# A cleared tile and a wait after every gather of node rows in a four-layer graph network

## The reference, cut to what matters

```python
edge_index = jnp.stack([src, dst])
h = jnp.maximum(_layernorm(x, axis=-1), 0.0)
x = x + _L0_gnn_ref(h, L0_gnn_weight, src, dst, edge_type_16)   # one matrix per edge type, summed by dst
h = jnp.maximum(_layernorm(x, axis=-1), 0.0)
x = x + _L1_gnn_ref(h, edge_index, L1_gnn_Wl, L1_gnn_Wr, L1_gnn_b)   # mean of neighbours, 3 steps
...
x = x + _L2_gnn_ref(h, L2_gnn_weight1, L2_gnn_weight2, src, dst)     # rows scaled by degrees
...
x = x + _L3_gnn_ref(h, edge_index, ...)                              # attention over neighbours, 2 steps
return x
```

## Time and profile before

| What | us |
|---|---|
| Median of three runs | 6565.89 |
| The three runs | 6560.53 to 6572.52 |
| Span of the profiled execution, first to last instruction | 8635.1 |
| Busy in it: DVE / POOL / PE / ACT | 4326.1 / 4305.3 / 4016.2 / 2282.2 |

### The profile page before, as it was taken

The page is one execution under the profiler, slowest core; times in us unless marked ns, Lnnn a source line. Parts: engine busy times, 40 slices in busy tenths (PEclk is TensorE's granted clock), DMA queues, the critical chain, the costliest instruction groups (busy, mean ns, idle before and its releaser), DMA issues. The chain is left out here.

```text
span 8635.1 us, 76490 instructions
## 1 busy us (share of the span) xinstructions
PE 4016.2 (47%) x19708; PEld 2671.9 (31%) x19708; DVE 4326.1 (50%) x14882; ACT 2282.2 (26%) x5999; POOL 4305.3 (50%) x4026
## 2 busy tenths in 40 slices
PE   1111158312888825654563664342465476567000
PEld 0000034101555514443442443332344355233000
DVE  3010069301999944434432553565244698677553
ACT  0000000001777621110110333354111133799000
POOL 5777720575000046546555674774555100888577
PEclk8555589655999955555555555555666666798555
DMA  1111100000222222222222343343122144555222
GB/s 42 47 46 47 47 19 0 21 1 5 103 113 107 99 70 79 69 73 64 69 68 63 112 128 112 94 139 112 44 68 68 77 161 163 125 146 138 76 82 77
DMA packets 413612, 684.96 MB, mean 79 GB/s; under 512 B 283685, under 2 KB 290444, under 8 KB 407978
## 3 DMA queue, kind: packets, MB, share of 16 engines
q1 hardware_dynamic: 282410, 542.14, 17.7%
q0 software_dynamic: 130944, 140.05, 7.5%
HBM read 310.94 MB, written 373.78 MB: 79 GB/s over the span
## 5 line engine op out<-in xcount | busy, mean ns | idle before, releaser
L711 POOL DMA_INDIRECT G<-states,srcq x1568 | 1678.9, 1071 | 851.1 <-issue 479.5
L1133 DVE TENSOR_TENSOR_SCAN R<-same,R,G 128x28 f32<-128x28 f32 x4480 | 883.8, 265 | 622.1 <-issue 499.9
L1793 PE MATMUL PS<-ident,HH 128*128 128x128 f32 x2357 | 529.8, 376 | 1257.4 <-ACT AT L2063 373.2
L2063 ACT COPY AT<-PS 128x512 f32<-128x512 f32 (+1 forms) x494 | 283.7, 581 | 2467.3 <-remote 1375.1
L1793 PEld LDWEIGHTS PS<-ident,HH 128*128 128x128 f32 x2357 | 402.8, 205 | 1332.9 <-issue 409.9
L711 POOL DMA_INDIRECT EE<-node_info,srcq x392 | 394.4, 1006 | 545.0 <-DMA node_info<-XC 415.7
L1701 PE MATMUL PS<-R 128*128 128x392 f16 x784 | 283.0, 361 | 673.2 <-remote 375.7
L711 POOL DMA_INDIRECT G<-states,srci x392 | 406.7, 1038 | 321.0 <-ACT HH L2161 199.1
L1808 PEld LDWEIGHTS PS<-WD,AT 128*128 128x128 f32 x2358 | 505.8, 316 | 183.0 <-issue 182.7
L1808 PE MATMUL PS<-WD,AT 128*128 128x64 f32 x2358 | 560.6, 416 | 0.0
L824 POOL DMA_INDIRECT out_nodes<-O,dstq x392 | 430.9, 1099 | 188.2 <-issue 123.3
(11 more groups left out here) (412 smaller groups left out, 10157.6 us busy)
## 6 DMA issues: line engine op xcount, KB each, us to landing
states<-O SPq DMA_DIRECT2D x70, 896.0 KB, 3.6
HH<-states SPq DMA_DIRECT2D x56, 896.0 KB
total<-R SPq DMA_DIRECT2D x56, 896.0 KB
XB<-resid SPq DMA_DIRECT2D x42, 896.0 KB
states<-HH SPq DMA_DIRECT2D x28, 896.0 KB, 3.9
G<-states,srcq POOLq DMA_INDIRECT x1568
resid<-XB SPq DMA_DIRECT2D x28, 896.0 KB
xl_of_src<-O SPq DMA_DIRECT2D x14, 1792.0 KB
```

What stands on the lines that cost most here:

```text
L711: return pool.indirect_dma_start(to, None, table_, bass.IndirectOffsetOnAxis(ap=idx, axis=0), bounds_check=bound, oob_is_err=False).then_i ...
L1133: last = dve.tensor_tensor_scan(out=out_[:, order, f], data0=flags[:, order], data1=in_[:, order, f], initial=initial[:, f:f + 1], op0=ALU ...
L1793: last = pe.transpose(PS[:, 4 + k, q * P:(q + 1) * P], HH[:, b, (g * G4 + q) * D2:(g * G4 + q + 1) * D2], ident[:])
L2063: act.copy(AT[:, k, 0:n * P], PS[:, 4 + k, 0:n * P]).then_inc(s_copied, 1)
```

## The change

A spare tile of 64 columns (32 KB, 256 bytes in each partition) is made. After each of the 784 gathers of node rows and each of the 392 gathers of node records GpSimd clears it and waits, with `step`, until the clearing is done, before it goes on to the next gather. That is 1176 clearings and as many waits. Nothing reads the tile. The gathers of the layers are as they were.

```diff
@@ -148,6 +148,7 @@
         fw = sb("fw", [P, 2, 6, HCOLS])
+        idle = sb("idle", [P, 64])
@@ -713,6 +714,9 @@
+            def pause():
+                step(pool.memset(idle[:], 0.0))
+
@@ -792,6 +796,7 @@
                 for j in range(PC):
                     at = turn % PCHUNKS * PC + j
                     gather(PG[:, b, j * D:(j + 1) * D], x, idx[:, at:at + 1], N - 1, s_pg[b])
+                    pause()
                     if j == PC // 2 and turn:
                         keep_rows(turn - 1)
```

## The result

The changed kernel takes **7335.84 us** (median of 4 runs, 7320.55 to 7341.27), the kernel before, run beside it, 6564.61 us (4 runs, 6560.53 to 6572.52). The ratio is 1.1174, with a 95% interval of 1.1158 to 1.119: 771 us slower (760 to 781). The forecast was 7319 us.

A forecast was written before the change was run, and what follows sets the result against it. The prediction took GpSimd's line of gathers to bound the preparation before layer 0, and added 1176 pauses of 0.64 us, 753 us, to the median 6566 us, giving 7319 us, range 6760 to 7570 us.

The forecast's parts named there:

- No stretch in the timed runs: Before layer 0, the trace's slowing of DVE beside GpSimd's gathers, 1480 us, was taken to be absent from the timed runs.
- The balance of the parts: Whole kernel without the stretch: 1630 us before layer 0 + 5527 - 559 = 6598 us, 0.5% from the median.
- GpSimd's line bounds the preparation, DVE's some tens of us to either side: Before layer 0, GpSimd's gathers end at 1625 us and set its start; DVE's line arrives together, at about 1630 us.
- the 50 us kept for that: Before layer 0: if DVE's line is now the later one, up to 50 us of the pauses is absorbed.
- The clearing, 0.14 us, right behind the gather: In each pause on GpSimd, clearing 64 columns takes 0.14 us and starts at once at the gather's end.
- The wait, 0.80 us instead of 0.30: In each pause, the next gather starts 0.80 us after the clearing's end, against 0.30 us between gathers today.
- The sum, 0.64 us x 1176 = 753 us: On GpSimd's line before layer 0, the period grows from 1.30 to 1.94 us, all on the path; chance 0.72.
- What else could be late: Edge stage: destinations' rows land at 891 us, DVE's last sum at about 1746 us, hidden under GpSimd's 2378 us.
- The SBUF port at nothing: Clearings beside DVE's histogram wait for none of its operations: nothing added; rival with 97 us more, 7416 us, chance 0.05.
- The cheap wait: Rival: the next gather is prepared ahead as far as the wait; 0.21 us a pause, 6813 or 6763 us; chance 0.14.
- The relief of a stretch: Rival: the stretch is real in timed runs and pauses let the histogram run under the gathers; 5883 us, chance 0.06.
- the hidden pause: Rival: DVE's timed line ends past 2378 us, so the pauses cost nothing; 6566 us, chance 0.03.

The follow-up runs named there:

- the second profile of before: The kernel before, unchanged, profiled once more: 6569.48 us, span 6567.8 us.

## Why the prediction was right

The forecast held: 7319 us, measured 7335.84. By its steps:

- **No stretch in the timed runs.** Right. The balance of the parts that led there came out well partly because two errors cancelled: it put layer 0 at 1633 us and all behind it at 4968, and the second profile of before shows 1723.6 and 4843. The record-keeping of the profile alone does not make the stretch: the profile of after and those of the nine experiments, with the same kind of records, have spans like their timed runs. That agrees with the Trainium skill, "NOTIFIC — the notification-queue block", section "10. Constraints, capacities, measured rates", by which a trace record costs the engine no cycles. What stretched that one execution is not known.
- **GpSimd's line bounds the preparation, DVE's some tens of us to either side.** Right, and the side is settled: DVE ended 47.7 us earlier. So nothing of the change was absorbed, and the 50 us kept for that were not needed. The line itself was mis-sized: 1625 us were forecast for its end and 2378 after the change, and DVE goes on at 1699.6 and 2463.3, 75 and 85 us later. Beside the edge stage the gathers do not keep 1.30 us, in the kernel before 35 us among the records and 16 among the destinations' rows; that stands below. The error is nearly alike in both kernels and falls out of the difference but for 10 us. DVE's line was put too short as well: the histogram, forecast to end at 597 us, ends at 636, since beside gathers it does not keep the pace that it has alone.
- **The clearing, 0.14 us, right behind the gather.** Right in place, 0.17 us in size.
- **The wait, 0.80 us instead of 0.30.** Right: 0.79 us, as in the earlier trace rows. The rows on a gather released by another engine's signal gave the price of one released by its own engine's. The experiments show what is dear about it: left to queue, a clearing of 0.12 us costs nothing and one of 0.17 us 0.03 us. With the wait for the newest instruction the distance to the next gather is 0.79 us, and the clearing stands in the open besides. That the next gather is made ready meanwhile in the one case, and not in the other, is inferred from these distances and from the store, which needs only 0.30 us behind the same wait; the making ready itself has no row in the profile.
- **The sum, 0.64 us x 1176 = 753 us.** The rows give 0.66 (1.96 against 1.30), and 0.17 + 0.30 = 0.47 where a store stands behind the pause, as the store of before follows its gather at once: 1120 x 0.66 + 56 x 0.47 = 766 us. Layer 0 moved by 763.7 us, the time by 771. So close an agreement is in part luck: in gaps of over 1 us and in gathers held up by DVE, which the rows leave out, the kernel after loses some 15 us more and 9 us less.
- **What else could be late.** The destinations' rows were late, as forecast (the first sum at 938.4 us, put at about 900), and DVE's last sum, put at 1746 us, came at 1783.4, hidden under 669.6 us of waiting.
- **The SBUF port at nothing.** Right for GpSimd's line, where 7 ns a clearing make 2 us; but clearing and histogram do not leave each other alone. One byte lost 74 ns beside the histogram, and 64 columns delayed DVE by 15 to 23 us, hidden under its wait. The Trainium skill has a rule of exclusion in "SBUF — State Buffer", section "Who interferes with whom", by which the forecast would have been 7416 us. These runs agree with it in that each side can hold the other up, not in that price.
- **The rivals.** The cheap wait (0.21 us a pause) is refuted by the row of 0.79 us. What it described is the price behind a wait of something other than a gather: the store behind a pause starts after 0.30 us. The relief of a stretch fell with the stretch (the pauses relieve the histogram by 24 us with one byte, on a line that nobody waits for), and the hidden pause with DVE's 47.7 us.

## What to carry to other kernels

In this kernel a wait for GpSimd's own newest instruction between two indirect gathers cost 0.6 us a gather, and the same instruction without it, or waited for one pause later, next to nothing. Before costing such an edit, ask which engine's line the following stage waits for, by the wait at that stage's entrance. And if a span is far from the timed runs, take the profile again before any of its durations is used.

## What the runs showed of the hardware that was not expected

**A gather can be held up by DVE.** In the second profile of before, 16 of the 392 gathers of records take over 1.5 us, and each lies beside one of the 16 sums of two 128 x 1792 tiles that DVE does in that time. One of them in the timeline of all engines:

```profile
1197.34 1.00 POOL L711 DMA_INDIRECT EE<-node_info,srcq  x1 [0.30 <-issue]
...
1198.57 2.02 DVE L1191 TENSOR_TENSOR XC<-XC,R 128x1792 f32<-128x1792 f32 x1
1198.65 2.81 POOL L711 DMA_INDIRECT EE<-node_info,srcq  x1 [0.30 <-issue]
```

The gather that starts 0.08 us into the sum ends 0.87 us after it. The 16 gathers lose 21.7 us in all (their durations above 1.0 us), and four gaps of 1.8 to 5.9 us add 13: this is why the records' period is 1.39 us on the mean ((1690.5 - 1145.7) / 391) and not the 1.30 of the forecast. Twelve gathers of the destinations' rows, each begun during such a sum, lose 15.7 us in the same way. In the first profile of before, whose longest gather of records took 1097 ns, this could not be seen: the sums of line 1191 start at 2215.9 us there, behind the last gather of records at 2095.3.

**A short clearing's length is mostly a fixed part.** Behind the histogram one byte took 116 ns in the mean, 64 columns of four bytes 166 ns and 512 columns 538 ns: some 0.8 ns a column ((166 - 116) / 63 and (538 - 166) / 448) on top of some 115 ns.
